# Macaron block with 16-head causal attention: two V products at once in every second step

## What is computed

```python
x = x + 0.5 * ffn(layernorm(x))      # silu(x wg) * (x wu), times wd; hidden width 384
x = x + attn(layernorm(x))
x = x + 0.5 * ffn(layernorm(x))
```

```python
q, k, v = x wq, x wk, x wv           # each to 16 heads x 64, q and k rotated
scores = einsum('bhid,bhjd->bhij', q, k) * 64 ** -0.5, -inf above the diagonal
out = einsum('bhij,bhjd->bhid', softmax(scores), v)
out = (heads side by side) wo        # back to width 128
```

## Time and profile before

| what | value |
|---|---|
| median of 3 runs | 1445.92 us |
| the profiled execution | 1444.78 us, span 1443.1 us |
| TensorE matmul | 1339.4 us busy (93%), 6048 instructions |
| VectorE | 946.9 us busy (66%) |
| GpSimd | 770.9 us busy (53%) |
| ScalarE | 635.5 us busy (44%) |
| mean granted TensorE clock | 0.948 of full speed |
| V products (L553), all | 1536 instructions |

### The profile page before, as it was taken

One profiled execution on the slowest core, in us unless ns is written; L12 is line 12 of the kernel. 1 busy time (PEld: TensorE's weight loads), 2 busy tenths in 40 slices (PEclk: granted clock), 3 DMA queues, 4 the chain that ended last, 5 costly groups with the idle time before them and its releaser, 6 DMA issues. The chain is left out here.

```text
span 1443.1 us, 24729 instructions
## 1 busy us (share of the span) xinstructions
PE 1339.4 (93%) x6048; PEld 737.6 (51%) x6048; DVE 946.9 (66%) x2046; ACT 635.5 (44%) x1240; POOL 770.9 (53%) x518
## 2 busy tenths in 40 slices
PE   5885799999999999999999999999999999999898
PEld 2543454545455555545454545554545454545355
DVE  5654667677767676777667667766776777774154
ACT  3663144444444443444343434443434344443474
POOL 4123266665656565656566666565656666565400
PEclk9997599999999998999999999999999999999899
DMA  7023545454545454545445453535354545444000
GB/s 278 18 85 102 141 112 148 100 152 96 150 103 147 111 147 111 146 113 132 120 110 147 109 149 85 152 93 153 86 150 96 151 95 151 96 107 94 0 22 37
DMA packets 113611, 165.85 MB, mean 115 GB/s; under 512 B 13360, under 2 KB 63408, under 8 KB 113456
## 3 DMA queue, kind: packets, MB, share of 16 engines
q1 hardware_dynamic: 113584, 165.53, 45.0%
HBM read 37.29 MB, written 10.49 MB: 33 GB/s over the span
## 5 line engine op out<-in xcount | busy, mean ns | idle before, releaser
L874 POOL TENSOR_TENSOR psum_p<-psum_p,shared_a 128x256 f32<-128x256 f32 (+1 forms) x192 | 281.0, 1464 | 354.2 <-ACT shared_a L669 350.9
L669 ACT ACTIVATE shared_a<-bank 128x512 f32<-128x512 f32 (+3 forms) x512 | 205.9, 448 | 300.1 <-PE bank L542 279.6
L745 DVE CUSTOM_DVE_ANT_0 max_scratch<-bank,tri_mask 128x128 f32<-128x128 f32 (+3 forms) x512 | 243.1, 486 | 128.2 <-PE bank L530 126.4
L542 PE MATMUL bank<-q_hm,k_l 65*128 65x512 f32 (+3 forms) x768 | 307.1, 400 | 0.0
L539 PE MATMUL bank<-q_hl,k_hh 128*128 128x512 f32 (+3 forms) x768 | 278.0, 362 | 0.0
L530 PE MATMUL bank<-k_hh,q_hl 128*128 128x512 f32 (+3 forms) x768 | 248.3, 378 | 7.5 <-DVE max_left L741 5.0
L741 DVE TENSOR_REDUCE max_left<-bank 128x1 f32<-128x512 f32 x256 | 175.1, 684 | 60.7 <-PE bank L530 60.5
L553 PE MATMUL bank<-shared_a,v_cur 128*64 128x512 f32 (+3 forms) x1024 | 208.1, 485 | 0.0
L530 PEld LDWEIGHTS bank<-k_hh,q_hl 128*128 128x128 f32 x768 | 137.5, 192 | 135.8 <-DVE max_left L741 59.0
L669 ACT ACTIVATE probs_more<-bank 128x512 f32<-128x512 f32 (+1 forms) x256 | 133.0, 568 | 156.4 <-PE bank L542 112.6
L725 DVE TENSOR_TENSOR terms<-bank,cos 128x512 f32<-128x512 f32 x124 | 85.5, 689 | 165.7 <-PE bank L504 165.7
(11 more groups left out here) (128 smaller groups left out, 1747.8 us busy)
## 6 DMA issues: line engine op xcount, KB each, us to landing
q_hl<-parts SPq DMA_DIRECT2D x256, 128.0 KB, 2.8
k_hh<-parts SPq DMA_DIRECT2D x256, 128.0 KB, 2.7
xn_cur<-xn_scratch SPq DMA_DIRECT2D x16, 1024.0 KB, 6.6
k_l<-parts SPq DMA_DIRECT2D x64, 256.0 KB, 4.3
q_hm<-parts SPq DMA_DIRECT2D x64, 256.0 KB, 5.1
v_cur<-shared_b SPq DMA_DIRECT2D x32, 512.0 KB, 6.1
w_qk<-w_scratch SPq DMA_DIRECT2D x32, 256.0 KB, 3.1
w_scratch<-first_w_parts SPq DMA_DIRECT2D x8, 512.0 KB, 3.1
```

What stands on the lines that cost most here:

```text
L542: nc.tensor.matmul(scores[h][:, x0:], k_l1[u][h][:, j * P:(j + 1) * P], q_hm[u][h][:, q], start=False, stop=True).then_inc(scores_full, 1)
L669: nc.scalar.activation(probs_of(s)[:, h, x0:], scores[h][:, x0:], ACT.Exp, scale=SCORE_SCALE).then_inc(probs_done, 1)
L745: nc.vector.tensor_tensor_reduce(out=max_scratch[k % 2][:, 0:w], in0=max_bank[k % 2][:, 0:w], in1=tri_mask[:, CHUNK - w:], scale=1.0, scal ...
L874: last = nc.gpsimd.tensor_tensor(acc, acc, new, ALU.add)
```

## The change

V products are made in odd steps alone, for two steps at once: in step s those of steps s - 3 and s - 2, one behind the other. Sums, normalisation, output projection and the addition to x move one step back each, so that the sums still follow a V product. The first projection of a pair moves from step 1 to step 0. The tables of max units change. GpSimd's and SyncE's lists stay as they are.

```diff
-        MAX_AHEAD = {3: (0,), 4: (3,), 5: (6, 7), 6: (8, 9), 7: (11, 12), 8: (14,), 9: (15,), 10: (18,), 11: (21, 22)}
-        MAX_BEHIND = {3: (1, 2), 4: (4, 5), 6: (10,), 7: (13,), 9: (16, 17), 10: (19, 20)}
+        MAX_AHEAD = {3: (0, 1), 5: (6, 7), 6: (8, 9), 7: (10, 11), 8: (14,), 9: (15, 16), 10: (19, 20), 11: (21, 22)}
+        MAX_BEHIND = {3: (2, 3), 4: (4, 5), 7: (12, 13), 9: (17, 18)}
...
-        PROJ_AT = {1: 0, 2: 1, 6: 2, 7: 3}
+        PROJ_AT = {0: 0, 2: 1, 6: 2, 7: 3}
...
+        SUM_AT, NORM_AT, OUT_AT, ADD_X_AT = (7, 3), (8, 4), (9, 5), (10, 6)
...
-                    if s == 4 and has_prev:
+                    if s == OUT_AT[1] and has_prev:
                         project_out(p - 1, i - 1 + u, 1 - u, 1)
-                    if s == 8:
+                    if s == OUT_AT[0]:
                         project_out(p, i, u, 0)
-                    if s >= LAG:
-                        times_v(p, u, s - LAG)
-                    elif has_prev:
-                        times_v(p - 1, 1 - u, s - LAG + NS)
-                    if s == 2 and has_prev:
+                    for back in (LAG + 1, LAG) if s % 2 else ():
+                        if s >= back:
+                            times_v(p, u, s - back)
+                        elif has_prev:
+                            times_v(p - 1, 1 - u, s - back + NS)
+                    if s == SUM_AT[1] and has_prev:
                         sum_probs(p - 1, 1)
-                    if s == 6:
+                    if s == SUM_AT[0]:
                         sum_probs(p, 0)
```

More of the change, by code:

```diff
@@ L789, in pair @@
                                 max_of(p + 1, k)
-                    if s == 3 and has_prev:
+                    if s == NORM_AT[1] and has_prev:
                         normalise(p - 1, 1)
-                    if s == 5 and has_prev:
+                    if s == ADD_X_AT[1] and has_prev:
                         add_to_x(p - 1, (2 * i + u - 1) // PAIRS, 1)
-                    if s == 7:
+                    if s == NORM_AT[0]:
                         normalise(p, 0)
-                    if s == 9:
+                    if s == ADD_X_AT[0]:
                         add_to_x(p, i // (PAIRS // 2), 0)
```

## The result

The changed kernel takes **1452.28 us** (median, 1450.75 to 1456.3), the kernel before 1447.95 us on the same chip (1444.32 to 1450.51): ratio 1.0036, 95% interval 1.0025 to 1.0047. It is slower by 0.3 to 0.5%, where the forecast was 1.1% faster. The time lies inside the range, on the wrong side.

A forecast was written before the change was run, and what follows sets the result against it. TensorE is busy 93%, but a chain through GpSimd and VectorE ends the odd pairs. Even pair 0, odd pair -0.45, with the clock -1.0 us a loop, x 16 = -16 us: 1430 us, range 1400 to 1489.

The forecast's parts named there:

- The form of the array: TensorE's V products: going to the 64-column form and back costs 0.35 us; six fewer blocks save 2.0 us a pair.
- rival D: The 0.35 us belongs to each V product, not the change of form, so joining saves nothing: 1475 us; chance 0.02.
- Second stretch: Step 9's scores to the next transposition, set by the chain: 13.81 (even) and 14.34 us (odd) become 15.2.
- First stretch: Transposition to step 9's scores, TensorE's: 1.3 us less in all, 20.55 us in odd pairs and 21.2 in even.
- Two waits come in: First stretch: unit 0 waits 0.6 us for fills; ScalarE's `invert` makes scores of steps 5 and 9 wait some 0.6.
- the forecast's own terms at full clock: Sum of both stretches without the clock: even pair 0, odd pair -0.45 us, over 16 loops.
- The clock: TensorE's stop in step 1 stays about 2.8 us; the low clock behind it costs 2.5 us a loop, hiding unit 0's 0.6.
- First and last pairs: Attention's edges: no term of their own; -1.0 us a loop was taken for all 16 loops.
- A: Rival: `join_max` falls behind GpSimd's sum of step 1 in even pairs too; 1489 us, or 1449 without second clock fall; chance 0.22.
- B: Rival: in odd pairs' step 8 GpSimd's sum of step 9 comes between the two `split` instructions; 1457 us; chance 0.19 alone.
- C: Rival: the chain has unseen slack, so TensorE's saving mostly arrives; 1385 to 1410 us, 1400 taken; chance 0.14.
- the case I gave 0.05: Whole kernel: gain and loss cancel, leaving the time about unchanged; chance 0.05.

The follow-up runs named there:

- Run 7: The kernel before with the second half of the rotation one step earlier (three table entries): 1379.38 us, ratio 0.953.
- run 6: The changed kernel with the second half of the rotation one step earlier (three table entries): 1387.35 us, ratio 0.9582.
- run 5: The changed kernel with eleven products that nothing reads put into TensorE's stop ahead of the transposition in even pairs: 1440.16 us, ratio 0.9953.
- run 4: The kernel before with eleven products that nothing reads put into TensorE's stop, ahead of unit 25 in even pairs: 1415.31 us, ratio 0.9772.
- runs 1: The changed kernel with the first projection and its `rope` back in step 1, behind `join_max`: 1473.31 us, ratio 1.0174.
- run 12: The changed kernel with VectorE's `rope` of the first projection behind the join, TensorE's projection left in step 0: 1479.44 us, ratio 1.0227.

## Why the prediction was wrong

**The form of the array: right.** Run 7 has the pieces. A unit followed by a lone V product, and what follows it; then a unit that no V product follows:

```profile
374.15 0.40 PE L530 MATMUL bank<-k_hh,q_hl 128*128 128x512 f32 x1
374.48 1.08 PE L553 MATMUL bank<-shared_a,v_cur 128*64 128x512 f32 x4
375.49 0.74 PE L530 MATMUL bank<-k_hh,q_hl 128*128 128x512 f32 x2
```

```profile
359.62 0.40 PE L530 MATMUL bank<-k_hh,q_hl 128*128 128x512 f32 x1
359.86 1.02 PE L572 MATMUL bank<-head_out,wo_cur 128*128 128x512 f32 x2
```

The unit takes 0.33 us in place of 0.24, the product 1.01 in place of 0.86. A score behind a V product takes 0.1 us more than another one. Sum 0.34. A 128-column V product alone, from its start to the next:

```profile
360.81 0.44 PE L553 MATMUL bank<-shared_a,v_cur 128*64 128x128 f32 x4
361.18 0.50 PE L530 MATMUL bank<-k_hh,q_hl 128*128 128x128 f32 x2
```

In run 6 such a product with one of 512 columns behind it:

```profile
414.16 1.30 PE L554 MATMUL bank<-shared_a,v_cur 128*64 128x128 f32 x8
415.39 0.56 PE L531 MATMUL bank<-k_hh,q_hl 128*128 128x512 f32 x2
```

1.23 - 0.37 = 0.86: the second product costs its bare work. So the 0.35 us stood, and rival D falls.

**Second stretch: right.** Forecast 15.2 in both pairs; at full clock 15.0 (run 5, even) and 15.2 (odd).

**First stretch: the step that failed.** It read "2.5 us less. Two waits come in", priced these at 0.6 us each, and ended at -1.3 us (-1.4 in even pairs). In the odd pair 21.28 was measured, not 20.55. In the even pair, with filler in both kernels so that the clock is full, the scores of step 9 come 707.59 - 684.90 = 22.69 us after the transposition before, and 719.76 - 697.17 = 22.59 after: a gain of 0.1, forecast 1.4. The sum missed 0.7 + 1.3 = 2.0 us a loop. Over 16 loops that is 32 us, about the distance from the -7 us of the forecast's own terms at full clock (-0.45 x 16) to the 24.9 measured. The saving of 2.5 us was right; the waits were not. They are found by going through the starts of run 5 against runs 4 and 6.

The wait for the fills: from the last scores of step 3 to the V products, in run 5 and, where nothing waits for the fills, in run 6:

```profile
700.84 0.28 PE L540 MATMUL bank<-q_hl,k_hh 128*128 128x256 f32 x1
...
702.50 1.72 PE L554 MATMUL bank<-shared_a,v_cur 128*64 128x512 f32 x8
```

```profile
393.86 0.28 PE L540 MATMUL bank<-q_hl,k_hh 128*128 128x256 f32 x1
...
394.55 1.73 PE L554 MATMUL bank<-shared_a,v_cur 128*64 128x512 f32 x8
```

1.66 - 0.69 = 1.0 us, forecast 0.6.

A wait that was not in the working at all is that of the first V projection, in step 8, which shares its bank with the last projection of step 7:

```profile
718.95 0.38 PE L513 MATMUL bank<-w_v,xn_cur 128*128 128x256 f32 x1 [0.60 <-DVE terms L734]
```

(run 5; the kernel after has it 15 times.) In the kernel before, an output projection and the V product of step 6 stood between the two and covered `rope`; here with filler, run 4:

```profile
705.45 1.02 PE L572 MATMUL bank<-head_out,wo_cur 128*128 128x512 f32 x2
706.40 0.44 PE L553 MATMUL bank<-shared_a,v_cur 128*64 128x128 f32 x4
706.77 0.38 PE L512 MATMUL bank<-w_v,xn_cur 128*128 128x256 f32 x1
```

The change moves both to step 9. From unit 14, 0.17 us of work, to the V projection 718.95 - 718.00 = 0.95 us pass: 0.8 us, forecast nothing, in even pairs alone.

The rest lies in steps 4 and 5, where units 2 to 5 now follow with only scores between them:

```profile
706.45 0.22 PE L531 MATMUL bank<-k_hh,q_hl 128*128 128x128 f32 x1
706.83 0.38 PE L531 MATMUL bank<-k_hh,q_hl 128*128 128x256 f32 x1 [0.15 <-DVE max_all L753]
707.10 0.50 PE L540 MATMUL bank<-q_hl,k_hh 128*128 128x512 f32 x1
```

Units 4 and 5 take 0.65 us where 0.18 would do (384 columns at the 0.23 us for 512). Unit 5 waits for its bank, which VectorE is still reading, and the scores of step 5 wait for the exponentials, which come behind `invert`: 0.6 us together. In the odd pair there are 0.25 us more ahead of the scores of step 9 (unit 14 at 761.76, scores at 762.19). The forecast had 0.6 for `invert`. So the waits are 1.0 + 0.6 + 0.8 = 2.4 us in even pairs and some 1.9 in odd ones, where the forecast had 1.2. I had listed what left the stretch and priced it as gain; I had not asked of each piece what it had covered. No run takes the wait of the V projection away, so its price is read from the trace and not tested.

**The clock: the second step.** The low clock behind the stop was taken as unchanged at 2.5 us a loop, of which it gives back 0.6 by hiding the wait of unit 0. It was 2.4 us (run 4) and is 0.9 now, so it gives back 1.5. About 1.0 of that is the wait for the fills: with a low clock, unit 0 comes late enough not to wait in even pairs, and they take 38.2 us against 37.6 with filler, where the kernel before took 38.1 against 36.5. The other part is that the longer even pairs, 39 us and more, were half of them before and are two of 14 now; why is open, since the stop is as long. Without this miss in the other direction the kernel would have come out some 12 us slower; that the two misses nearly cancel is luck.

**First and last pairs: counted like the loop, and that was wrong.** The sum took all 16 loops alike. From the first transposition of the last maxima to the fifth the kernel after takes 7.2 us more (157.7 for 150.5), and behind the last one 2.5 us more (148.1 for 145.6), while the loop between comes out 1 us shorter. So the loss of the whole kernel lies here. The first pair has no V products ahead of unit 0, so it meets the fills early, where no wait of unit 0 is seen before:

```profile
179.27 0.50 PE L531 MATMUL bank<-k_hh,q_hl 128*128 128x128 f32 x2 [2.02 <-DMA k_hh<-parts]
```

**Rivals.** A did not come: the join takes 0.15 to 0.2 us in the loop. It was close, 0.09 us, and runs 1 and 12 show it when the join moves forward instead, where I looked for it only with the join moving back. The join of run 12 started 0.56 us after the sum and ended with it, 1.27 us for 0.15. The Trainium skill ("SBUF — State Buffer", "Who interferes with whom") says that a VectorE instruction with two SBUF inputs contends with a GpSimd instruction that reads SBUF, and the trace agrees. B came once, at the start (the two `split` of step 8 took 3.44 us in place of 1.36). C falls: the stop is as long as before, and the chain sets the second stretch. What came is nearest to the case I gave 0.05, gain and loss cancelling.

## What to carry to other kernels

When work is moved out of a stretch, ask of each piece which latency it was covering (a bank being read, exponentials, a DMA), and price the uncovered wait beside the work saved. Where a chain through other engines sets the period, shorten the chain first: here three table entries gave 65 to 68 us, and only behind them did the saving on TensorE become worth anything (9 us, and only with `rope` behind the join). When experiments move two engines' work by one table, give each its own table, or a bank wait hides what is asked.

## What the runs showed of the hardware

A stop of TensorE of 2.65 us once in 75 us cost 2.3% of the whole time through the clock that fell behind it; filling the same stop with 11 products that nothing reads took that back, though it shortened no wait. And an instruction made ready earlier can end later: the join that was asked for 1.2 us sooner met GpSimd's sum and took 1.27 us in place of 0.15.
